# Attention scores on three shared PSUM banks, two banks for VectorE, preparation in one block, and half-width taps in a four-stage transformer kernel

## The reference

```python
x = L0_attn_x
x = x + _L0_attn_ref(_layernorm(x), ...)   # delta rule: 16 heads of 64, conv of 4 taps, gated state
x = x + _L0_ffn_ref(_layernorm(x), ...)    # shared expert + one of 8 experts per token
x = x + _L1_attn_ref(_layernorm(x), ...)   # window attention, 16 heads of 8, window of 64
x = x + _L1_ffn_ref(_layernorm(x), ...)    # full attention over 256 tokens, then 2 of 8 experts
...
# window attention: softmax over the last 64 keys, then Wo
scores = jnp.einsum('blhd,blwhd->blwh', q, k_win) * dh ** (-0.5)
out = jnp.einsum('blwh,blwhd->blhd', jax.nn.softmax(scores, axis=2), v_win) ; out @ Wo.T
# full attention: h = layernorm(x, g, b); qkv = h @ w_qkv + b_qkv
attn = jax.nn.softmax(jnp.einsum('bqhd,bkhd->bhqk', q, k) / np.sqrt(DK), axis=-1)
x = x + einsum(attn, v) @ w_o + b_o
```

## Time and profile before

| | |
|---|---|
| median of 3 runs | 6774.56 us (6771.26 to 6777.18) |
| the profiled execution | 6762.3 us, span of its instructions 6760.5 us |
| busy over the span | PE 86%, PEld 65%, DVE 55%, ACT 49%, POOL 37% |
| first instruction of the window stage | 4519.28 us |
| first normalised tile of its loop | 4576.26 us |
| last instruction of its loop | 5310.63 us |
| first normalised tile of the full stage's loop | 5362.77 us |

### The profile page before, as it was taken

One profiled execution on the slowest core, in us unless ns is written; L12 is line 12 of the kernel. 1 busy time (PEld: TensorE's weight loads), 2 busy tenths in 40 slices (PEclk: granted clock), 3 DMA queues, 4 the chain that ended last, 5 costly groups with the idle time before them and its releaser, 6 DMA issues. The chain is left out here.

```text
span 6760.5 us, 187448 instructions
## 1 busy us (share of the span) xinstructions
PE 5798.9 (86%) x67109; PEld 4366.6 (65%) x67110; DVE 3719.7 (55%) x7246; ACT 3294.8 (49%) x7154; POOL 2518.8 (37%) x2359
## 2 busy tenths in 40 slices
PE   5999999999999999999999996757888588885586
PEld 4676676666766766667667665555666466664486
DVE  5555555555555555555555555554444466665443
ACT  2555555555555555555555552232333255552165
POOL 5545444544454445454544453340000100003553
PEclk9999999999999999999999998889999799996598
DMA  3000000000000000000000001120000000001124
GB/s 95 21 22 18 18 22 22 18 18 22 21 18 18 21 22 18 18 21 22 18 18 22 22 18 33 30 72 1 0 0 0 2 0 0 0 0 38 37 62 122
DMA packets 99340, 161.01 MB, mean 24 GB/s; under 512 B 19973, under 2 KB 82245, under 8 KB 96069
## 3 DMA queue, kind: packets, MB, share of 16 engines
q1 hardware_dynamic: 76260, 121.44, 6.0%
q0 software_dynamic: 14080, 26.64, 1.2%
q10 hardware_dynamic: 8320, 4.19, 0.2%
HBM read 118.03 MB, written 104.87 MB: 33 GB/s over the span
## 5 line engine op out<-in xcount | busy, mean ns | idle before, releaser
L789 PE MATMUL bank<-wc,hT 128*128 128x512 f32 x2088 | 1043.4, 615 | 47.3 <-issue 28.7
L956 PE MATMUL bank<-X,kqe 128*128 128x64 f32 x6240 | 775.7, 278 | 75.0 <-DVE rb L1451 54.5
L956 PEld LDWEIGHTS bank<-X,kqe 128*128 128x128 f32 x6240 | 727.8, 192 | 99.1 <-DVE rb L1451 70.1
L1189 ACT ACTIVATE TT<-bank 128x512 bf16<-128x512 f32 x640 | 382.3, 597 | 664.0 <-PE bank L937 661.6
L1491 DVE TENSOR_TENSOR yb<-bank,masks 128x512 bf16<-128x512 f32 x768 | 526.3, 686 | 179.8 <-PE bank L919 172.5
L789 PEld LDWEIGHTS bank<-wc,hT 128*128 128x128 f32 x2088 | 352.4, 191 | 310.2 <-issue 282.0
L1289 POOL TENSOR_TENSOR qa<-qa,qt 128x512 f32<-128x512 f32 x390 | 486.9, 1269 | 34.8 <-POOL qt L1284 34.8
L1430 DVE TENSOR_TENSOR kqe<-bank,ex 128x512 f32<-128x512 f32 x520 | 335.1, 686 | 274.8 <-PE bank L863 274.8
L1189 ACT ACTIVATE T<-bank 128x512 bf16<-128x512 f32 x640 | 348.9, 595 | 272.1 <-PE bank L930 270.2
L1322 POOL TENSOR_SCALAR_AFFINE_SELECT kqe<-kqe 128x512 f32<-128x512 f32 x260 | 215.7, 830 | 642.5 <-DVE kqe L1430 642.5
L919 PEld LDWEIGHTS bank<-T,mTb 128*128 128x128 bf16 x6144 | 264.2, 99 | 263.9 <-ACT T L1189 106.0
(11 more groups left out here) (531 smaller groups left out, 13256.5 us busy)
## 6 DMA issues: line engine op xcount, KB each, us to landing
sent_l0f<-blank_l0f SPq DMA_DIRECT2D x64, 528.0 KB
sent_l1m<-blank_l1m SPq DMA_DIRECT2D x64, 528.0 KB
xin<-sent_l1m SPq DMA_DIRECT2D x139, 66.0 KB
taken_l1m<-back_l1m SPq DMA_DIRECT2D x16, 512.0 KB, 8.7
xin<-sent_l0f SPq DMA_DIRECT2D x75, 66.0 KB
decay_sums<-decay_rows SPq DMA_DIRECT2D x264, 3.0 KB
cw_stage<-in_L_attn_conv_w_dram SPq DMA_DIRECT2D x4, 1024.0 KB, 6.4
out_dram<-x_sb ACTq DMA_DIRECT2D x8, 512.0 KB, 7.0
```

Of the source, the lines that this page charges most:

```text
L789: mm = pe.matmul(bk[:, :], src[:, j:j + P], w["wc"][:, j, at * 512:(at + 1) * 512], start=(j == 0), stop=(j == TAPS - 1))
L956: mm = pe.matmul(bk[:, i * D0:(i + 1) * D0], lhsT(hh), rhs(hh), start=True, stop=True)
L1189: nc.scalar.activation(dst, bk[:, :].rearrange("p (h a u) -> p h a u", h=8, u=1 << l), ACT.Copy).then_inc(actb.done.sem, 1)
```

## The change

Four parts:

1. In both attentions `sc` becomes banks (2, 3, 4, 1), `st` stays 2 to 5, so three banks are shared and the waits read `filled - 1`: three of four maxima, three of four exponentials. Bank 0 goes to `dv`, which now has two banks.
2. On TensorE `project_out` (J) moves from behind I to between G and H, and where t = 1 `turn_h` moves ahead of `turn_back`.
3. The preparations become one block: the loads, the statistics, the transposes and the constants of each attention share it. The memsets move from VectorE to GpSimd, the copies from VectorE to ScalarE. The powers for tiles 0 to 3 are taken there, those of later tiles in a new GpSimd loop beside the attention's loop.
4. In the delta stage tap 2 and tap 3 of "v1" and the gate chunk "z1" are cut in two halves of 256 columns, the first of which moves forward.

```diff
-            def taps(b, src, ch, first, count):
+            def taps(b, src, ch, first, count, half=None):
+                cols = slice(0, 512) if half is None else slice(half * 256, half * 256 + 256)
...
                         for G in range(2):
+                            if l == 2 and G == 1:
+                                taps(b, hT[t % 2], "v1", 3, 1, 0)
                             join_a(b, t, l, G)
                             if l > 1:
                                 join_tt(b, t, l - 1, G)
+                            if l == 1 and G == 1:
+                                taps(b, hT[t % 2], "v1", 2, 1, 0)
                             if step:
                                 solve(b, t, step, G)
                             if l == 4:
-                                gate_tap(b, f"z{G}")
+                                gate_tap(b, f"z{G}", 0 if G == 1 else None)
...
                         if l <= 2:
-                            taps(b, hT[t % 2], "v1", l + 1, 1)
+                            taps(b, hT[t % 2], "v1", l + 1, 1, 1)
                         if l == 4:
                             turn_h(b, t + 2, "h")
+                            gate_tap(b, "z1", 1)
...
-        sc = Ring(ctx, nc, f"scores_{tag}", [bank[i] for i in (2, 3, 0, 1)], SF * U, ahead=SF + 4)
+        sc = Ring(ctx, nc, f"scores_{tag}", [bank[i] for i in (2, 3, 4, 1)], SF * U, ahead=SF + 4)
...
-        dv = Ring(ctx, nc, f"to_dve_{tag}", bank[7:8], 16, ahead=4)
+        dv = Ring(ctx, nc, f"to_dve_{tag}", [bank[7], bank[0]], 16, ahead=4)
...
-                    pe.wait_ge(st.done.sem, st.done.at(b, st.filled - 2))
+                    pe.wait_ge(st.done.sem, st.done.at(b, st.filled - 1))
...
-                pe.wait_ge(sc.done.sem, sc.done.at(b, sc.filled - 2))
+                pe.wait_ge(sc.done.sem, sc.done.at(b, sc.filled - 1))
...
-                    turn_back(b, u - 1)
                     if t == 0:
+                        turn_back(b, u - 1)
                         queries(b, 1)
                     else:
                         turn_h(b, TPB * (u // TPB + 3))
+                        turn_back(b, u - 1)
...
                     scores(b, u + 2, 0)
+                    project_out(b, u - 1)
                     weigh(b, u)
                     pe.wait_ge(dv.done.sem, dv.done.at(b, dv_use(u, "top")))
                     turned_scores(b, u + 1, 0)
-                    project_out(b, u - 1)
...
+        @block.gpsimd
+        def _(pool):
+            start_signals(pool, scales_ready)
+            with pool.Fori(0, bodies) as b:
+                if mid is None:
+                    pool.tensor_tensor(mr[:, 1, bass.ds(b * U + U, U)], var[:, 0, bass.ds(b * U + U, U)],
+                                       c["halves"][:, 0:U], ALU.pow).then_inc(scales_ready.sem, 1)
...
+                        if u == 0:
+                            dve.wait_ge(scales_ready.sem, scales_ready.at(b, 1))
                         norm_h(b, turn + 2, am_use(u - 1, "hT") if u else 4)
```

In `norm_stats` the new pieces run beside the statistics, and GpSimd takes the powers of four columns alone:

```diff
+                    if i == 0 and sync:
+                        sync(sp)
...
+        if scalar:
+            block.scalar(scalar)
+        if tensor:
+            block.tensor(tensor)
...
+            for i in range(1 if later else 2):
+                T = slice(0, 2 * TPB) if later else slice(i * half, (i + 1) * half)
```

More of the change, by code:

```diff
@@ L2692, in attention_stage @@
         mr = sb("mr", [P, 2, tiles + BEHIND])
[L2694 to L2698 removed]
+        mean = None if mid is None else sb("mean", [P, 2, 1 + tiles + U])
+        var = sb("variance", [P, 2, tiles + U])
         h = sb("h", [P, TPB, P])
@@ L3150, in window_stage @@
              "last_v": last_v}
-        attention_stage(nc, c, x_all, None, w, tiles, "win", True, take)
+        attention_stage(nc, c, x_all, None, w, loads, tiles, "win", True, take)
 def full_stage(nc, c, x_all, mid_all, a, tiles):
```

263 lines of the change are left out of this document (134 added, 129 removed).

## The result

The kernel after takes 6881.4 us (median of four runs, 6876.9 to 6884.2), the kernel before 6775.9 us beside it (four runs, 6771.3 to 6779.3). The ratio is 1.0157, with a 95% interval of 1.0142 to 1.0172. The prediction was 6697 us, faster: wrong in sign. The profiled execution of after has a span of 6875.0 us, 114.5 more than the 6760.5 of before.

A forecast was written before the change was run, and what follows sets the result against it. It took TensorE to bound the delta loop and the chain of engine handovers the full loop. Terms -42 -25 -19 -35 +44 = -77 on 6774.6 gave 6697 us; main case 6675 to 6720, range 6655 to 6742.

The forecast's parts named there:

- parts 1 and 2, full loop: Full attention loop: waiting for three of four results lengthens the pair of units from 23.02 to 24.4 us, 44 us more.
- rival (c): Full loop: new waits' idle time lowers TensorE's clock; 25% of its work at half clock gives 150 us more, 6850; chance 0.06.
- The chain itself: Full loop: summed steps of a unit from one engine to the next, 12.09 and 12.3 us, a pair of 24.4.
- the chain has no place for the gift: Full loop: argument that the second dv bank and moved projection cannot give back what the third shared bank costs.
- Window loop: Window attention loop: projection moved under VectorE's maxima, less 0.60 us for a third maximum; 19 us less, bounds 0 and 63.
- Delta stage: Delta loop: first halves of taps 2 and 3 fill two TensorE waits, 0.66 us a tile over 64 tiles, 42 us less.
- the 50 us: Delta loop: alternative gain of some 50 us, if halving a tap costs next to nothing, by the Trainium skill's rule.
- Rival (a): Delta loop: its waits come back elsewhere, a chain through ScalarE holding TensorE; total change -35, 6740 us; chance 0.14.
- Preparations: Before both attention loops: one block, moved work hidden under VectorE's statistics; 25 us less in window stage, 35 in full.
- (b): Full loop: pays nothing for the third bank, second dv bank and moved projection repay it; total change -121, 6654 us; chance 0.11.
- (d): Preparations: give only half, since a copy or load outlasts the statistics; total change -47, 6727 us; chance 0.11.
- Experts stage: Experts stage: no term in the sum, 0 us of change predicted.

The follow-up runs named there:

- e2: Kernel before with only the two waits changed, from two of four results to three; ratio 1.0307, full loop 956.9 us.
- e6: Kernel after with extra TensorE products that nothing reads ahead of its long waits in both loops; ratio 0.9917, full loop 826.3 us.
- e7: Kernel after with old banks and waits, new order kept, plus extra unread products ahead of waits in both loops; ratio 0.9755, full loop 752.2 us.
- e10: Kernel before with extra unread products in the full loop alone; ratio 0.9966, full loop 767.9 us.
- e3: Kernel after with TensorE's old order, new banks and waits kept; ratio 1.003, window loop 701.7 us, full loop 951.4 us.
- e11: e6 with one bank for VectorE again, and in the window loop old banks and waits and one more extra product; ratio 0.9883, full loop 829.7 us.
- e1: Kernel after with both attention loops put back as before, new preparation and halves kept; 6635 us beside 6736, ratio 0.9839.
- e8: Kernel before with tap 2 of v1 alone in halves; single run of 6760 us, no ratio, delta stage 14 us shorter.
- e5: Kernel after with the full loop of before, the window loop in old order with new banks and waits, gate chunk whole; ratio 0.9816.
- e4: Kernel after with old banks and waits, TensorE's new order kept; ratio 0.9895, window loop 762.4 us, full loop 796.3 us.
- e9: e5 with the full loop in new order plus two extra unread products a pair; 6592 us beside 6768, ratio 0.9736.

## Why the prediction was wrong

**The step that failed** is the term "parts 1 and 2, full loop", +44 us, measured +202. It was worked out at one clock throughout. The two waits alone cost 166 us in e2, of which 73 are chain; in after it is 58 of chain and 164 of clock. The loss that follows from the same waits through the clock stood only as rival (c), with a chance of 0.06. The full loop of before already averaged 0.97, 10 of its 32 pairs were disturbed, and I added some 4 us of waits to each pair. The evidence I set against it, gaps of 0.5 us in the delta loop at 1.00, was about other gaps: there they are single and short, here two waits of 1.1 us stand 2 us apart. That the distance is what makes the difference was not tested. Rival (c) gave 150 us for a quarter of the work at half clock; at a mean of 0.78 the loop paid 164.

**The term in its parts.** Undisturbed pair 24.79 (e6) against 22.98 of before: 1.81 x 32 = 58 us of chain. After's mean pair of 29.92 less 24.79: 5.13 x 32 = 164 us of clock. Before's mean of 23.59 less 22.98: 20 us of clock that it paid as well. 58 + 164 - 20 = 202. That the clock's part is caused by idle time is shown by three doses in the same kernel: no filling 0.78 and 29.9 us, about half 0.89 and 27.3, all 0.99 and 24.8; and by e7 and e10 with the old waits. The Trainium skill ("TensorE: Matmul & The Clock Gate", A second HAM failure mode: psum-queue depth-cycling) describes a clock that swings because TensorE is idle for short times between groups while it cycles through banks; the rows agree with the idle times, and e6 adds that the cycling alone does not do it, since the same rotation of banks ran at 0.99 once the waits were filled.

**The chain itself** was right in its mechanism and 14 us small. In e6 A to D is 3.10 us (I had 3.11), D to G 2.79 (2.79), G to the next A 6.40 (6.19). Nearly the whole difference is the projection between G and H: 0.64 us (5717.73 to 5718.37) where I estimated 0.44. But the sum counted the moved projection as a cost alone. With the same waits and the old order the pair at full clock is 25.27 us (e2), so the new order gains 0.48 us a pair. What it removes stands in e2's timeline, a wait of the keys for VectorE's sum of the projection. With the second bank and the old order it is gone too; these are the keys in e2 and then in e3:

```profile
5860.76 1.13 PE L2771 MATMUL bank_full<-hT_full,wk_full 128*128 128x256 f32 x4 [0.52 <-DVE mid L3072]
```

```profile
5683.94 1.03 PE L2838 MATMUL bank_full<-hT_full,wk_full 128*128 128x256 f32 x4
```

So "the chain has no place for the gift" of a second bank is shown by e11 for the new order, which has removed this wait already. With the old order there is a place for it.

**Window loop**, -19 predicted, +4.4 measured. The undisturbed pair fell from 21.90 to 21.43, so -15 us at full clock: near the forecast by luck, since its parts were wrong. The gain that I gave to the moved projection comes as well from the second bank, which I had priced at nothing. The two don't add (banks alone 21.09, order alone 20.66, both 21.43): the 0.51 us wait ahead of the keys is gone with either. Why both together come out above the banks alone was not settled. The mean pair of after is 22.28 us, single ones up to 26, which is 27 us above the undisturbed pair in all: 14 of them are the waits without a releaser ("What else disturbs the window loop"), some 13 are left for the clock, and before paid 5. The sum left out both. Why banks alone run at 0.99 with waits of 0.9 us stays open; it was not tried to fill other waits there one by one.

**Delta stage**, -42 predicted, -44.1 measured (-48.2 in e1, the same code); tap 2's half gives the 0.32 us (e8), the gate's halves nothing (e5), as written. A half costs 0.51 us (2058.10 to 2058.61), two of them 1.02 against 0.94 for a whole tap, so halving costs 0.08. The rule of the Trainium skill ("TensorE: Matmul & The Clock Gate", Back-to-back issue gap), by which halving costs almost nothing, does not fit that price exactly, and the 50 us estimated from it are about as near to these two as my 42. Rival (a) fell.

**Preparations**, -25 and -35 predicted, -25.6 and -35.0 measured; what was moved stayed hidden under the statistics. Rivals (b) and (d) fell.

**Experts stage**, 0 predicted, +12.8: the change does not touch its code. Its clock was 0.76 and 0.85 in its second and third 40 us, against 1.00 and 0.91 before. From the end of the delta stage to the window's first tile the experiments with the new preparation took 415 to 426 us, after 428: that it is chance in the clock is likely, not shown.

## What to carry to other kernels

Price a new wait on TensorE twice: once as the time on the chain, and once as what the clock does to the work around it. In the full loop of after the second price was 2.8 times the first (164 against 58 us); in the window loop of e2, which stood at 0.98 before, the same two waits cost 40 us on the chain and next to nothing through the clock. So a mean clock below 1.00 is a warning, and no forecast. Look at the single waits in the timeline and at how close together they stand, not only at their share of the loop. Where such waits can't be removed, products that nobody reads, put into a bank that is free anyway, can be the cheapest repair (167 us here), and they are a quick test of whether the clock is the cause. When one change offers two remedies, ask whether they remove the same wait: each of the two paid alone in the window loop's pair, and together less than either. And when a repair doesn't bring what it should, look whether the long pairs really run at a low clock; in the window loop several did not.

## What the hardware showed

- The granted clock does not follow the sum of the idle time. The window loop of e3 has TensorE busy 84% of the time and runs at 0.99; that of e4, with the same products, has the shorter undisturbed pair (20.66 us against 21.09), and runs at 0.91. In e3's pair the three waits of 0.9 us stand over 5 us apart (they end at 4881.40, 4886.55 and 4897.66); in e4's one of 1.44 and one of 0.68 us end within 1.6 us of each other. That this is the reason is not shown.
- More work made a loop faster: 448 added records, 167 us less.
- In the full loop of after the disturbance is regular: the lengths of the pairs repeat every eight (27.9, 30.6, 30.5, 30.6, 27.8, 30.6, 28.1, 32.8 us), and four runs of after lie within 0.11%. The loss is a steady cost of this code.
- TensorE can stand idle with no engine to wait for, in some passes of a loop and not in others: in after's window loop six such waits of 1.3 to 3.1 us make 14 us, with packets on the instruction queue shortly before; e3 and e9 have neither. That the one causes the other is likely, not shown.
